# Mixing stage of a MetaFormer layer: the sum of squares on GpSimd beside VectorE's sum, and GpSimd's setup of later stages behind the stage

## The chip, the cores and the metric

One core of one Trainium2 chip. The metric is the device time of one execution in microseconds (us); a profiled execution also gives the span from the first to the last instruction.

## What is computed

x has 384 x 384 tokens with 128 channels. The layer normalises x, makes five projections of it (left, left gate, right, right gate, output gate), mixes left and right over the grid channel by channel, normalises the result over the channels, projects it, and adds it to x. A second part (an expert-choice FFN: per expert the 8 best tokens) follows.

```python
left  = (xn @ Wl + bl) * sigmoid(xn @ Wlg + blg)
right = (xn @ Wr + br) * sigmoid(xn @ Wrg + brg)
out = einsum('bkjd,bkid->bijd', left, right) / n        # per channel d: 384x384 @ 384x384
out = layer_norm(out, on_a, on_b) * out_gate            # over the 128 channels of a token
x = x + out @ Wo + bo
```

The layer norm of `out` needs, for each of the 147456 tokens, the sum and the sum of squares over the 128 channels. The change is about these two sums.

## The kernel before

The instruction streams are written by hand, one block for each engine, with semaphores between them. There are three stages and a tail.

**Stage 1** (144 steps of 1024 tokens) normalises, transposes and projects, and writes left, right and gate to DRAM by channel. GpSimd works here on normalisation (L618) and on the low parts of the input (L624).

**Mixing stage** (128 channels, buffers of two). A channel is a 384x384 map, on chip as 128 partitions x 1152 numbers. Per channel d:
- SyncE loads right and left (L485, L486), two channels ahead, when the low halves of channel d - 2 are done, and stores the mixed map (L497).
- ScalarE rounds right and left to their high parts (L811, L813). VectorE subtracts these from the whole to get the low parts (L1020, twice).
- TensorE multiplies high x high, low x high and high x low, 27 matmuls of 128x384 (L1342), into three of six PSUM banks.
- ScalarE reads the banks twice: the map itself (`mix`, L828) and its square (`mixsq`, L829). It waits first until the sums of channel d - 2 are done, since `mix` and `mixsq` have two buffers.
- VectorE adds `mix` to sum1 (L1039) and `mixsq` to sum2 (L1041). All three operands lie in SBUF.

Within a step VectorE's order is: both low halves of channel d + 1, then both sums of channel d - 1. ScalarE's order is: both casts of d + 1, then both readings of d - 1.

**Between the stages** VectorE makes mean, variance and 1/deviation out of sum1 and sum2, in three thirds of 128x384, and splits both into three bf16 parts each (L1059 to L1084). SyncE stores the parts to DRAM (L551) and loads them back broadcast for **stage 3** (L518), where TensorE applies them as outer products (L1366) and VectorE's `weighted` (L1103) begins.

**GpSimd's setup.** After stage 1 GpSimd prepares constants for what follows, each operation waiting for the one before (`alone`, which counts s_pool0): a memset and nine small loads of `exact`, then sel, half_off (two), rowsign, b2_row, pick_row, statrow (4096 bf16 in each partition, L657), coef, two affine selects on sel, one on rowsign, and two iotas (L666, L668). 17 counts in all. Then it waits for VectorE's split_rows (s_setup) and issues three loads of coef (L673). VectorE's split_rows, in the last step of the mixing stage, and SyncE's loads of gb_col and b2_row (L546, L548), behind the mixing stage and in front of the first store of the parts, both wait for all 17. During the mixing stage GpSimd does nothing.

Of the kernel before, what the change touches and what calls it, by code (L numbers as in the profile page):

```python
# [28 lines left out]
ALU = mybir.AluOpType  # L29
# [8 lines left out]
PARTS = 3  # L38
# [75 lines left out]
def build(nc, x, norm_a, norm_b, Wl, bl, Wr, br, Wlg, blg, Wrg, brg, Wog, bog, on_a, on_b, Wo, bo,  # L114
# [26 lines left out]
    with ExitStack() as ctx:  # L141
# [3 lines left out]
        def sem(name):  # L145
            return ctx.enter_context(nc.semaphore(name))
# [216 lines left out]
        s_ev = sem("s_ev")  # L363
        s_acc = sem("s_acc")
        s_mst = [sem(f"s_mst{b}") for b in range(2)]
        s_msq = sem("s_msq")
# [78 lines left out]
        N_EXACT = 3 * PARTS  # L445
        N_FIRST = 3
        N_POOL0 = 17

# [145 lines left out]
        def _(pool):  # L594
# [52 lines left out]
            for q in range(PARTS):  # L647
                pool.dma_start(exact[q:q + 1, 0, :], on_a.rearrange("(o d) -> o d", o=1)).then_inc(s_exact, 16)
                pool.dma_start(exact[PARTS + q:PARTS + q + 1, 0, :], on_b.rearrange("(o d) -> o d", o=1)).then_inc(s_exact, 16)
                pool.dma_start(exact[PARTS + q:PARTS + q + 1, 1, :], bo.rearrange("(o d) -> o d", o=1)).then_inc(s_exact, 16)  # L650
            alone(nc.gpsimd.memset(sel[:, :], 0.0))
            alone(nc.gpsimd.memset(half_off[0:EXPERTS, :], 0.0))
            alone(nc.gpsimd.memset(half_off[EXPERTS:P, :], float(CHUNK)))
            alone(nc.gpsimd.memset(rowsign[:, :], 1.0))
            alone(nc.gpsimd.memset(b2_row[:, :], 0.0))
# [4 lines left out]
            for shift in (0, EXPERTS):  # L660
                alone(nc.gpsimd.affine_select(out=sel[:, :], in_=sel[:, :], compare_op=ALU.not_equal, fill=1.0,
                                              base=-shift, pattern=[[-1, EXPERTS]], channel_multiplier=1))

            alone(nc.gpsimd.affine_select(out=rowsign[:, 0:1], in_=rowsign[:, 0:1], compare_op=ALU.is_ge, fill=-1.0,
                                          base=-PARTS, pattern=[[0, 1]], channel_multiplier=1))
            alone(nc.gpsimd.iota(place[:, :], pattern=[[1, STEPS * TOP]], base=0, channel_multiplier=0,  # L666
# [90 lines left out]
        def _(act):  # L757
# [64 lines left out]
            def evacuate(i, b):  # L822
                d = 2 * i + b
                act.wait_ge(s_mst[b], 16 * i)
                act.wait_ge(s_acc, mark(1, d - 2, 1))
                act.wait_ge(s_mix, mark(1, d, 1))
                mixed = banks[:, NT * b:NT * (b + 1), 0:GRID]
                nc.scalar.activation(mix[:, b], mixed, ACT.Copy, scale=1.0 / GRID).then_inc(s_ev, 1)  # L828
                nc.scalar.activation(mixsq[:, b], mixed, ACT.Square, scale=1.0 / GRID).then_inc(s_ev, 1)  # L829

# [105 lines left out]
        def _(dve):  # L936
# [8 lines left out]

            for s_, n in ((s_bn, 1), (s_var, 1), (s_xhat, 1), (s_prod, 4), (s_acc, 1),
                          (s_w3, 2), (s_r3, 1), (s_v3, 1), (s_m3, 2)):
                dve.sem_inc(s_, 2 * n)
# [63 lines left out]
            nc.vector.memset(sum1[:, :, :], 0.0)  # L1012
            nc.vector.memset(sum2[:, :, :], 0.0)

# [7 lines left out]
            def split_rows():  # L1022
                dve.wait_ge(s_gtp, 1)
                nc.vector.tensor_copy(gate_t[:, :], ps[7][:, 0:EXPERTS]).then_inc(s_setup, 1)
                dve.wait_ge(s_exact, 16 * N_EXACT)
                dve.wait_ge(s_pool0, N_POOL0)
                for q in range(2):
# [7 lines left out]
            def moments(i, b):  # L1035
                d = 2 * i + b
                dve.wait_ge(s_ev, mark(2, d, 1))
                dve.wait_ge(s_acc, mark(1, d - 1, 1))
                nc.vector.tensor_tensor(sum1[:, :, :], sum1[:, :, :], mix[:, b], ALU.add)  # L1039
                dve.wait_ge(s_ev, mark(2, d, 2))  # L1040
                nc.vector.tensor_tensor(sum2[:, :, :], sum2[:, :, :], mixsq[:, b], ALU.add).then_inc(s_acc, 1)  # L1041

# [12 lines left out]

            dve.wait_ge(s_acc, mark(1, DIM - 1, 1))
            for t in range(NT):
                dve.wait_ge(s_msq, t + 1)
# [422 lines left out]
```

## Time and profile before

| | us |
|---|---|
| median of 3 runs | 2883.23 (2879.32 to 2885.48) |
| profiled execution, its own time | 2879.22 |
| its span | 2877.5 |
| stage 1 | up to about 1144 |
| mixing stage, first to last addition to sum1 | 1164.59 to 1840.60 |
| stage 3 | from about 1870 to 2768 |

Times in the trace count from the start of the span. PE is TensorE's matmul, PEld its weight load, DVE is VectorE, ACT ScalarE, POOL GpSimd, SP SyncE. "L1041" is line 1041 of the kernel. Matmul ends are modelled, so a busy PE is not PE at its peak. A few per cent of the matmuls can be missing from a trace. An instruction's duration runs from its start to its end as recorded, so time that it spends waiting inside, for a port for instance, is part of it.

### The profile page before, as it was taken

The page shows a single profiled execution, that of the slowest core. Times are in us where ns is not written, and L with a number is a line of the kernel's source. Part 1 is how long each engine was busy: PE and PEld are TensorE (multiplying, and loading weights), DVE is VectorE, ACT ScalarE, POOL GpSimd, SP SyncE. Part 2 cuts the span into 40 slices and gives each one's busy share as a digit, 9 for nine tenths or more (in the row PEclk, how much of TensorE's full clock was granted, in tenths as well). Part 3 has the DMA queues.
Part 4 walks back from the last instruction along what each step waited for, and adds up shares of the span by engine and source line. Part 5 has one row for each costly group of instructions (what it writes and reads, how often), then busy time and mean ns, then how long its engine had stood idle before and what let it go on. Part 6 is the DMA issues. An engine that isn't in the chain of part 4 may idle for free.

```text
span 2877.5 us, 65085 instructions
## 1 busy us (share of the span) xinstructions
PE 2605.2 (91%) x14998; PEld 2144.7 (75%) x15070; DVE 2411.0 (84%) x4715; ACT 2254.2 (78%) x4283; POOL 1833.9 (64%) x1920
## 2 busy tenths in 40 slices
PE   7999999999999999999999999589899899988935
PEld 6888888888888887888888888566666666666623
DVE  6777777777777776999999999979899999988962
ACT  6888888888888887787778888568888888888840
POOL 7888888888888887000000000089999999999941
PEclk9999999999999999999999999789999999999978
DMA  5777777777776776999999999699999999999946
GB/s 197 273 270 266 268 273 270 268 265 272 272 269 263 272 272 248 327 332 329 320 324 332 332 331 337 229 336 374 364 365 373 366 373 365 372 355 359 365 147 214
DMA packets 281642, 873.08 MB, mean 303 GB/s; under 512 B 29710, under 2 KB 82080, under 8 KB 281600
## 3 DMA queue, kind: packets, MB, share of 16 engines
q1 hardware_dynamic: 270160, 854.87, 80.6%
q10 hardware_dynamic: 10800, 17.21, 2.0%
q0 software_dynamic: 640, 0.54, 0.2%
q8 instruction: 14, 0.23, 0.0%
q14 instruction: 28, 0.23, 0.0%
HBM read 492.97 MB, written 379.52 MB: 303 GB/s over the span
## 4 chain that ended last, share of the span: by engine, by line
PE 46%; DMA 18%; DVE 9%; issue 9%; POOL 8%; ACT 6%; SPq 3%; DVEq 1%; POOLq 0%; ACTq 0%
PE banks L1307 35%; DMA arena<-left_d 10%; DMA work<-gate_d 5%; PE banks L1296 4%; PE banks L1342 4%; POOL arena L686 3%; POOL arena L692 2%; ACT work L904 2%; PE banks L1393 2%; POOL rs L709 2%; ACT arena L828 2%; DMA work<-in_x_dram 1%; DVE bn L1123 1%; DVE arena L1114 1%; DVE arena L1041 1%
## 5 line engine op out<-in xcount | busy, mean ns | idle before, releaser
L1307 PE MATMUL banks<-x_parts,w_parts 128*128 128x512 f32 x4320 | 1067.4, 398 | 3.4 <-POOL x_parts L624 3.4
L1307 PEld LDWEIGHTS banks<-x_parts,w_parts 128*128 128x128 f32 x4320 | 791.2, 188 | 165.3 <-POOL x_parts L624 3.8
L1342 PE MATMUL banks<-left_parts,right_parts 128*128 128x384 f32 x3456 | 633.2, 342 | 58.4 <-ACT arena L829 51.0
L1342 PEld LDWEIGHTS banks<-left_parts,right_parts 128*128 128x128 f32 x3456 | 608.5, 191 | 82.8 <-issue 79.0
L982 DVE SCALAR_TENSOR_TENSOR arena<-banks,cols,arena 128x512 f32<-128x512 f32 x576 | 406.5, 747 | 247.4 <-ACT arena L794 244.3
L904 ACT ACTIVATE work<-arena,rs 128x128 f32<-128x128 f32 x1152 | 352.6, 388 | 126.6 <-POOL rs L709 126.6
L673 POOL DMA_DIRECT2D coef<-yt x3 | 1.5, 518 | 690.0 <-DVE yt L1033 690.0
L1375 PE MATMUL banks<-wo_sb,arena 128*128 128x128 f32 x2304 | 395.5, 300 | 6.3 <-DVE arena L1114 6.3
L686 POOL TENSOR_TENSOR arena<-arena,work 128x512 f32<-128x512 f32 x288 | 360.4, 1274 | 56.6 <-DVE arena L1103 56.2
L1375 PEld LDWEIGHTS banks<-wo_sb,arena 128*128 128x128 f32 x2304 | 359.9, 192 | 45.6 <-issue 16.7
L624 POOL TENSOR_TENSOR x_parts<-xn,x_parts 128x512 fp32r<-128x512 f32 x288 | 372.1, 1292 | 6.6 <-ACT x_parts L782 6.6
L618 POOL TENSOR_SCALAR arena<-arena,bn,rs 128x128 f32<-128x128 f32 x432 | 365.9, 856 | 0.5 <-POOL rs L611 0.5
L611 POOL TENSOR_TENSOR rs<-vv,mhalf 128x8 f32<-128x8 f32 x144 | 239.1, 1660 | 164.5 <-DVE vv L965 164.5
L800 ACT ACTIVATE arena<-banks,cols 128x512 f32<-128x512 f32 x288 | 198.5, 689 | 180.2 <-PE banks L1307 180.2
L1393 PE MATMUL banks<-yt,gate_t 128*64 128x512 f32 x576 | 214.0, 613 | 77.4 <-ACT yt L895 77.3
L972 DVE TENSOR_SCALAR arena<-arena,bn,rs 128x128 f32<-128x128 f32 x720 | 259.7, 438 | 5.7 <-POOL rs L611 5.4
L1376 PE MATMUL banks<-coef,statrow 128*128 128x128 bf16 x1152 | 253.4, 220 | 0.0
L709 POOL TENSOR_TENSOR rs<-vv,mhalf 128x8 f32<-128x8 f32 x144 | 237.6, 1650 | 6.5 <-DVE vv L1132 3.0
L811 ACT CAST right_parts<-arena 128x1152 fp32r<-128x1152 f32 x128 | 148.6, 1161 | 116.0 <-DMA arena<-right_d 88.4
L1103 DVE SCALAR_TENSOR_TENSOR arena<-work,cols,banks 128x512 f32<-128x512 f32 x288 | 201.0, 739 | 34.7 <-DMA work<-gate_d 19.8
L782 ACT ACTIVATE xn<-banks,cols 128x512 f32<-128x512 f32 x288 | 224.2, 779 | 2.0 <-PE banks L1296 2.0
L782 ACT ACTIVATE x_parts<-banks,cols 128x512 fp32r<-128x512 f32 x288 | 222.6, 773 | 0.0
(180 smaller groups left out, 4180.8 us busy)
## 6 DMA issues: line engine op xcount, KB each, us to landing
arena<-in_x_dram SPq DMA_DIRECT2D x144, 512.0 KB, 3.4
left_d<-arena SPq DMA_DIRECT2D x144, 512.0 KB, 2.6
right_d<-arena SPq DMA_DIRECT2D x144, 512.0 KB, 3.4
gate_d<-arena SPq DMA_DIRECT2D x144, 512.0 KB, 4.2
arena<-right_d SPq DMA_DIRECT2D x128, 576.0 KB, 5.7
arena<-left_d SPq DMA_DIRECT2D x128, 576.0 KB, 6.7
mixed_d<-arena SPq DMA_DIRECT2D x128, 576.0 KB, 4.3
work<-mixed_d SPq DMA_DIRECT2D x144, 512.0 KB, 4.8
```

The lines of the kernel that those rows point to most:

```text
L618: last = nc.gpsimd.tensor_scalar(xhat[:, b, t], xin[:, b, t], mean_of(b, t), rs[:, b, t:t + 1], ALU.subtract, ALU.mult)
L624: nc.gpsimd.tensor_tensor(x_parts[:, LO, b, c], xn[:, b, c], x_parts[:, HI, b, c], ALU.subtract).then_inc(s_lo, 1)
L686: nc.gpsimd.tensor_tensor(gated[:, b, h], gated[:, b, h], gt[:, b, h], ALU.mult).then_inc(s_g3, 1)
L709: nc.gpsimd.tensor_tensor(rs[:, b], vv[:, b], mhalf[:, 0:2 * TILES], ALU.pow).then_inc(s_n3, 1)
L782: last = nc.scalar.activation(dst, ps[c][:, :], ACT.Identity, bias=cols[:, B_COL:B_COL + 1], scale=cols[:, A_COL:A_COL + 1])
L904: last = nc.scalar.activation(ys[:, b, h, c], summed[:, b, h, c], ACT.Copy, scale=rs[:, b, k:k + 1])
L972: last = nc.vector.tensor_scalar(xhat[:, b, t], xin[:, b, t], mean_of(b, t), rs[:, b, t:t + 1], ALU.subtract, ALU.mult)
L982: nc.vector.scalar_tensor_tensor(out=dst[:, b, CHUNK * c:CHUNK * (c + 1)], in0=ps[bank][:, :], scalar=cols[:, col:col + 1], in1=sig[:, c], ...
L1307: last = nc.tensor.matmul(ps[2 + k][:, :], w_parts[:, wq, k], x_parts[:, xq, b, c], start=((wq, xq) == TERMS[0]), stop=((wq, xq) == TERMS[ ...
L1342: last = nc.tensor.matmul(ps[NT * b + t][:, 0:GRID], lr_parts[RIGHT][:, rq, b, k, t * P:(t + 1) * P], lr_parts[LEFT][:, lq, b, k], start=( ...
L1375: nc.tensor.matmul(ps[2 + h][:, tok], gated[:, b, h, tok], wo_sb[:, :], start=True, stop=False)
L1393: nc.tensor.matmul(ps[6 + b][EXPERTS * h:EXPERTS * (h + 1), :], gate_t[:, :], yt[:, b, h], start=True, stop=True).then_inc(s_l3, 1)
```

## The change

The sum of squares moves from VectorE to GpSimd, with a semaphore of its own (s_acc2); sum1 keeps s_acc. ScalarE's square of channel d waits for s_acc2 of d - 2, its plain reading for s_acc of d - 2 as before. GpSimd waits until VectorE has cleared sum2 (s_clr). The moments wait for both sums. GpSimd's setup, all but `exact` and rowsign, moves behind its 128 additions; split_rows now waits for the six counts that stand in front of them (N_ROWS), SyncE's loads of gb_col and b2_row still for all 17.

```diff
+        N_ROWS = 6
         N_POOL0 = 17
@@ GpSimd, behind the loads of exact
+            alone(nc.gpsimd.memset(rowsign[:, :], 1.0))
+            alone(nc.gpsimd.affine_select(out=rowsign[:, 0:1], in_=rowsign[:, 0:1], compare_op=ALU.is_ge, fill=-1.0,
+                                          base=-PARTS, pattern=[[0, 1]], channel_multiplier=1))
+
+            def squares(i, b):
+                d = 2 * i + b
+                pool.wait_ge(s_ev, mark(2, d, 2))
+                pool.wait_ge(s_acc2, mark(1, d - 1, 1))
+                settle(pool, s_tick_pool)
+                nc.gpsimd.tensor_tensor(sum2[:, :, :], sum2[:, :, :], mixsq[:, b], ALU.add).then_inc(s_acc2, 1)
+
+            def stage2(i):
+                for b in range(2):
+                    squares(i, b)
+
+            pool.wait_ge(s_clr, 1)
+            pairs(pool, DIM, stage2)
+
             alone(nc.gpsimd.memset(sel[:, :], 0.0))
...
-            alone(nc.gpsimd.memset(rowsign[:, :], 1.0))
...
@@ ScalarE, evacuate
                 nc.scalar.activation(mix[:, b], mixed, ACT.Copy, scale=1.0 / GRID).then_inc(s_ev, 1)
+                act.wait_ge(s_acc2, mark(1, d - 2, 1))
                 nc.scalar.activation(mixsq[:, b], mixed, ACT.Square, scale=1.0 / GRID).then_inc(s_ev, 1)
@@ VectorE
-            nc.vector.memset(sum2[:, :, :], 0.0)
+            nc.vector.memset(sum2[:, :, :], 0.0).then_inc(s_clr, 1)
...
-                dve.wait_ge(s_pool0, N_POOL0)
+                dve.wait_ge(s_pool0, N_ROWS)
...
-                nc.vector.tensor_tensor(sum1[:, :, :], sum1[:, :, :], mix[:, b], ALU.add)
-                dve.wait_ge(s_ev, mark(2, d, 2))
-                nc.vector.tensor_tensor(sum2[:, :, :], sum2[:, :, :], mixsq[:, b], ALU.add).then_inc(s_acc, 1)
+                nc.vector.tensor_tensor(sum1[:, :, :], sum1[:, :, :], mix[:, b], ALU.add).then_inc(s_acc, 1)
...
             dve.wait_ge(s_acc, mark(1, DIM - 1, 1))
+            dve.wait_ge(s_acc2, mark(1, DIM - 1, 1))
```

## Rows read from the trace of the kernel before

**Rows 1.** The page, part 1: busy us, share of the span, instructions.
```profile
PE 2605.2 (91%) x14998; PEld 2144.7 (75%) x15070; DVE 2411.0 (84%) x4715; ACT 2254.2 (78%) x4283; POOL 1833.9 (64%) x1920
```

**Rows 2.** Stretches: length; busy PE, PEld, DVE, ACT, POOL; clock, DMA share, GB/s.
```profile
1164.60:1840.60 676.00, 622.36 (x3407) 597.72 (x3406) 648.47 (x513) 547.82 (x505) 0.00 (x0) 0.98 0.94 327
1843.30:1870.00 26.70, 4.09 (x10) 1.55 (x11) 24.32 (x54) 9.20 (x20) 0.44 (x1) 0.50 0.42 146
```

**Rows 3.** Groups by line, 1150 to 1950: busy us, mean ns; idle before, releaser.
```profile
L1342 PE MATMUL banks<-left_parts,right_parts 128*128 128x384 f32 x3456 | 633.2, 342 | 58.4 <-ACT arena L829 51.0 <-ACT left_parts L813 7.0
...
L1020 DVE TENSOR_TENSOR left_parts<-arena,left_parts 128x1152 fp32r<-128x1152 f32 x128 | 173.2, 1353 | 1.1 <-ACT left_parts L813 0.5
...
L1041 DVE TENSOR_TENSOR arena<-arena 128x1152 f32<-128x1152 f32 x128 | 172.7, 1350 | 0.0
```

**Rows 4.** Timeline, VectorE, mixing stage: start us, us, engine, line, operation.
```profile
1164.59 1.35 DVE L1039 TENSOR_TENSOR arena<-arena 128x1152 f32<-128x1152 f32 x1
...
1186.21 1.35 DVE L1041 TENSOR_TENSOR arena<-arena 128x1152 f32<-128x1152 f32 x1
1187.48 1.35 DVE L1020 TENSOR_TENSOR right_parts<-arena,right_parts 128x1152 fp32r<-128x1152 f32 x1
...
1840.60 1.34 DVE L1039 TENSOR_TENSOR arena<-arena 128x1152 f32<-128x1152 f32 x1
```

**Rows 5.** Waits, 1250 to 1850: waiter, releaser, us in total, times, longest.
```profile
PE banks L1342 <- ACT arena L829: 45.3, 51, 2.6
```

**Rows 6.** Groups by line and shape, GpSimd, whole span.
```profile
L686 POOL TENSOR_TENSOR arena<-arena,work 128x512 f32<-128x512 f32 x288 | 360.4, 1274 | 56.6 <-DVE arena L1103 56.2
...
L681 POOL COPY rcol<-late 128x8 f32 x136 | 26.4, 194 | 0.0
...
L702 POOL COPY late<-mx 128x16 f32 x68 | 13.6, 200 | 0.0
...
L661 POOL TENSOR_SCALAR_AFFINE_SELECT sel<-sel 128x64 f32<-128x64 f32 x2 | 0.5, 240 | 0.3 <-POOL coef L658 0.2
...
L605 POOL TENSOR_SCALAR_AFFINE_SELECT ident<-ident 128x128 f32<-128x128 f32 x1 | 0.3, 290 | 0.2 <-POOL ident L604 0.2
```

**Rows 7.** Timeline: GpSimd and VectorE at the same time, in three places.
```profile
11.47 0.96 DVE L1001 TENSOR_TENSOR w_parts<-arena,w_parts 128x640 fp32r<-128x640 f32 x1
...
1860.23 0.56 DVE L1068 TENSOR_TENSOR arena<-arena 128x384 f32<-128x384 f32 x1
...
1860.40 0.44 POOL L681 COPY rcol<-late 128x8 f32<-128x8 f32 x1 [17.58 <-ACT late L850]
...
2770.01 1.42 DVE L1171 SCALAR_TENSOR_TENSOR late<-late,half_off 128x1152 f32<-128x1152 f32 x1 [0.95 <-ACT expo L876]
2770.78 1.44 POOL L736 TENSOR_SCALAR_AFFINE_SELECT work<-work 128x896 f32<-128x896 f32 x1
2771.47 1.37 DVE L1173 TENSOR_SCALAR late<-late,gb_col 128x1152 f32<-128x1152 f32 x1
```

**Rows 8.** Timeline: GpSimd's setup ahead of the mixing stage, and VectorE beside it.
```profile
1141.75 0.20 POOL L651 MEMSET sel<- 128x64 f32 x1
...
1142.90 3.51 POOL L657 MEMSET statrow<- 128x4096 bf16 x1
...
1144.56 1.93 DVE L1011 TENSOR_SCALAR gate_nat<-gate_nat,gsum 64x128 f32<-64x128 f32 x1
...
1147.96 1.10 POOL L666 IOTA late<- 128x1152 f32 x1
...
1149.13 2.16 POOL L668 IOTA late<- 128x1152 f32 x1
```

**Rows 9.** Timeline: behind the mixing stage, SyncE's issues and the next stage's first VectorE work.
```profile
1845.25 1.22 SPq L546 DMA_DIRECT2D gb_col<-in_L_ffn_gate_b_dram  x2
...
1854.40 0.41 SPq L551 DMA_DIRECT2D stat_d<-arena  x1
...
1870.02 1.40 DVE L1103 SCALAR_TENSOR_TENSOR arena<-work,cols,banks 128x512 f32<-128x512 f32 x2 [0.15 <-DVE arena L1069]
```

More of the change, by code:

```diff
@@ L364, in build @@
         s_acc = sem("s_acc")
+        s_acc2 = sem("s_acc2")
+        s_clr = sem("s_clr")
         s_mst = [sem(f"s_mst{b}") for b in range(2)]
@@ L662, in _ @@
                                               base=-shift, pattern=[[-1, EXPERTS]], channel_multiplier=1))
-            alone(nc.gpsimd.affine_select(out=rowsign[:, 0:1], in_=rowsign[:, 0:1], compare_op=ALU.is_ge, fill=-1.0,
-                                          base=-PARTS, pattern=[[0, 1]], channel_multiplier=1))
             alone(nc.gpsimd.iota(place[:, :], pattern=[[1, STEPS * TOP]], base=0, channel_multiplier=0,
@@ L943, in link @@
                 dve.wait_ge(s_dve, chain[0])
-            for s_, n in ((s_bn, 1), (s_var, 1), (s_xhat, 1), (s_prod, 4), (s_acc, 1),
+            for s_, n in ((s_bn, 1), (s_var, 1), (s_xhat, 1), (s_prod, 4), (s_acc, 1), (s_acc2, 1),
                           (s_w3, 2), (s_r3, 1), (s_v3, 1), (s_m3, 2)):
```

## The prediction

> **What bounds the kernel now.** I read the busy shares first [rows 1]: TensorE 91%, VectorE 84% of the 2877.5 us span. That is an average over three stages, so next comes the table by stretches [rows 2]; the mixing stage is its first line. In it VectorE is busy 648.5 of 676.0 us (96%), TensorE 92%, ScalarE 81%, the DMA engines 94%, GpSimd not at all. So three resources lie close together, and VectorE is the fullest. Then the groups of that stage [rows 3]: per channel VectorE does four additions or subtractions of 128x1152 (two low halves, the two sums), TensorE 27 matmuls (633.2 / 128 = 4.95 us). The timeline shows the additions following each other at 1.27 us (1186.21 to 1187.48), though one is listed with 1.35 [rows 4]. Four make 5.08 us. The first and the last addition to sum1 lie 1840.60 - 1164.59 = 676.0 us apart, 127 channels, so 5.32 us a channel. VectorE is 95% of that; TensorE waits for ScalarE's reading of its banks 51 times in 600 us of the stage, 45.3 us in all [rows 5].
>
> **What is removed and added in the mixing stage.** Removed from VectorE: one addition of 1.27 us in each of 128 channels; 3.81 us are left. Added on GpSimd: the same addition of 1152 elements. The trace has it only at 512 elements: 1.274 us [rows 6]. Bounds: in proportion 1152 / 512 x 1.274 = 2.87 us; with a fixed part as in GpSimd's copy of 16 elements (0.20 us, nearly all fixed), 0.20 + 1152 x (1.274 - 0.20) / 512 = 2.62 us. I take 2.62, since a fixed part is visible, and keep 2.87 as the upper end. By itself this fits twice into 5.32 us: GpSimd is idle, and nothing on its queue stands behind it.
>
> **Can the two engines add at the same time?** This decides the case, and two places of the trace speak of it [rows 7]. At 1860.40 GpSimd starts a copy of 8 elements, which takes 0.194 us elsewhere (136 times, [rows 6]); here it takes 0.44 and ends at 1860.84, just behind VectorE's subtraction of two SBUF tiles (1860.23 + 0.56 = 1860.79). At 2770.78 GpSimd starts an affine select of 896 elements. Its price from 64 elements (0.240) and 128 (0.290) [rows 6] is 0.290 + 768 x 0.00078 = 0.89 us; it takes 1.44. Had it begun to read only when VectorE's operation on two SBUF tiles ended (2771.43), it would have ended near 2772.2; it ended at 2772.22. So a VectorE instruction with two SBUF inputs keeps a GpSimd instruction that reads SBUF waiting. The other direction is less clear. At 2771.47 a VectorE operation with one input waits for the affine select (1.37 us for 1152 elements, ending 0.62 behind it). But the one subtraction with two inputs beside reading GpSimd work, at 11.47 [rows 7], took 0.96 us for 640 elements, against 0.82 on the line through 0.56 (384 elements) and 1.35 (1152): 0.14 longer.
> The Trainium skill, "SBUF — State Buffer", section "Who interferes with whom", has a rule against this change: a VectorE instruction with two SBUF inputs contends with a GpSimd instruction that reads SBUF, and whichever issues second is blocked until the first has finished. By that rule the third step below is a plain sum; by the 0.14 us of the row at 11.47 alone VectorE would lose almost nothing. The trace agrees with the rule where GpSimd is the one that waits; no row shows a long GpSimd addition against a VectorE addition.
> Whoever yields, additions that exclude each other cost their sum: 3 x 1.27 + 2.62 = 6.43 us a channel, above the 5.32 of now. With 0.05 us for each of two hand-overs (1860.84 - 1860.79) and some idling (now 5% of the period beside the fullest engine, then less, since TensorE and DMA have slack again), I take 6.65. Ends: 6.43 without any idling, and 3 x 1.27 + 2.87 + 0.10 = 6.78, with 5% idling 7.1. **Term: 127 x (6.65 - 5.32) = +169 us**; ends +141 and +226.
>
> **Waits added.** ScalarE's square of channel d now waits for GpSimd's sum of d-2; behind it on ScalarE stand the casts of a later channel, and TensorE waits for the square to free its banks. With 6.65 us a channel the sum of d-2 has a whole channel more, so this wait costs nothing unless GpSimd falls two channels back. GpSimd waits for VectorE's clearing of sum2, which comes before the first channel: nothing. VectorE's wait before the moments is now for both sums. Now the last square is followed by sum1 and sum2 (1840.60 to about 1843.2, 2.6 us); then 1.35 + 2.62 = 4.0, and up to one more 2.62 if GpSimd is a channel behind. **Term: +2 us** (0 to +5).
>
> **GpSimd's setup behind the stage.** Before the mixing stage it delayed VectorE once: a tensor_scalar of 64x128 issued at 1144.56 took 1.93 us and ended with GpSimd's memset of statrow (1142.90 + 3.51) [rows 8]. VectorE then still waits for the first channel's data, so taking that away gives nothing. Behind the stage the same operations (from 1141.75 to 1149.13 + 2.16 [rows 8], without rowsign's about 9.2 us of GpSimd) lie beside VectorE's chain of moments and splits, which fills 24.3 of 26.7 us [rows 2] and which sets the end of the stage: weighted (L1103) follows it at 1870.02 [rows 9]. The chain alternates operations with two inputs (0.56 us), which I let run beside a memset that only writes (no row shows it), with casts and tensor_scalars, which are held as the one at 1144.56 was. So the 3.51 us memset costs up to 3.51 - 0.56 = 2.9 us, and the two iotas (1.10 and 2.16 us, not shown beside VectorE) up to 0.5 and 1.6. **Term: +4.5 us** (0 if all is hidden, +9 if all is exposed).
> SyncE's queue passes its wait for the setup some 10 to 13 us behind the last sum instead of at once (L546 at 1845.25 now); six issues follow, two of which take 1.22 us, so an estimate of 3.7. The first store of the split rows (1854.40, 11.2 us behind the last sum [rows 9]) can come up to 5 us later, but the chain that makes it is itself later by 4.5, and what it feeds is needed only by L1103 at 1870.02. Nothing. The three coefficient transfers are issued behind the setup too, ahead of the first outer product: nothing. rowsign stays ahead of the stage.
>
> **Sum.** The profiled execution took 2879.2 us (span 2877.5). 2879.2 + 169 + 2 + 4.5 = 3054.7; the median of the runs lies 4.0 above the profiled one, so **3058 us**. With the ends of all terms: 2883 + 141 = 3024 to 2883 + 240 = 3123.
>
> **Rivals.**
> *They overlap (faster).* If GpSimd's addition runs beside VectorE's, as it does beside ScalarE, VectorE falls to 3.81 us, and the DMA share decides: 0.94 x 5.32 = 5.0 us, TensorE 4.95. With 5.05: 127 x -0.27 = -34, + 4.5 for the setup: about 2854 us. For it: the 0.14 us at 11.47. Against: both places where GpSimd waited to the end. It decides from the point where more than 6.43 - 5.32 = 1.1 of GpSimd's 2.62 us lie beside VectorE's additions; exactly there the time is that of now plus the setup, about 2890.
> *TensorE loses its clock, or GpSimd falls behind.* At 6.65 us a channel TensorE is busy 74%. The granted clock is 0.98 of full in the stage now, at 92% busy [rows 2]. At the lower of its two levels (1.2 GHz) 27 matmuls take some 9.9 us; with a fifth of the stage there, 127 x 0.2 x 3.25 = +83 on top: about 3140. The same follows if ScalarE comes to wait for GpSimd's sum of d-2, in whose time VectorE has nothing to add. Against: at the lower level TensorE would be busy without a break, and in the stage of now the clock comes back to a mean of 0.98.
>
> **Chances.** Additions exclude each other, 2985 to 3123: 0.74. Overlap, faster: 0.12. Overlap in part, within 2878 to 2985: 0.05. Clock or lag, above 3123: 0.09. The range must leave out no more than 0.2: 2930 to 3150 holds the first case, some 0.02 of the third and 0.04 of the last. A difference under 0.2% can't be told from none here. Faster 0.13, same 0.03, slower 0.84.
>
> **What would show it.** Right: GpSimd's additions in the mixing stage well above 2.62 us on average or VectorE's above 1.35; the fullest pair, VectorE and GpSimd, adds up to the period; DMA share and TensorE fall to about three quarters; a cast or tensor_scalar of the moments chain stretched to 3 us. Wrong: GpSimd at 2.6 to 2.9 and VectorE at 1.35 with a period near 5; or TensorE's clock well under 0.9 in the stage.

## The result and the profile after

The changed kernel takes 3006.81 us (median of 4 runs, 3005.52 to 3009.91), the kernel before, run beside it, 2884.36 us (4 runs, 2879.32 to 2890.04). The ratio is 1.0438, 95% interval 1.0417 to 1.0458: **slower by 4.4%, some 122 us**. The forecast was 3058 us, range 2930 to 3150, slower: the side and the mechanism came true, its main term was some 40% too large (+169 us against +119).

The page of after, part 1 (busy us, share of the span of 3008.2 us, instructions), against [rows 1]:
```profile
PE 2631.0 (87%) x15070; PEld 2148.2 (71%) x15070; DVE 2556.2 (85%) x4587; ACT 2254.5 (75%) x4283; POOL 2263.7 (75%) x2048
```
VectorE has 128 additions less (4587 instructions instead of 4715) and 145 us more of busy time. A VectorE instruction that GpSimd holds isn't listed as idle: it gets longer. That is the first thing to see, and a table of busy shares alone would mislead here, since VectorE looks no freer than before.

The table by stretches of after, the mixing stage (length; busy PE, PEld, DVE, ACT, POOL; granted clock, DMA share, GB/s), against the first line of [rows 2]:
```profile
1164.60:1950.00 785.40, 636.97 (x3388) 594.64 (x3387) 775.05 (x376) 544.78 (x502) 415.37 (x125) 0.98 0.82 280
```
VectorE is busy 775.05 of 785.40 us (99%, before 96%) with three additions a channel instead of four. TensorE falls from 92% to 81%, the DMA share from 0.94 to 0.82. The clock stays at 0.98.

Groups by line of after, 1150 to 2000 (busy us, mean ns; idle before, releaser), against [rows 3]:
```profile
L1360 PE MATMUL banks<-left_parts,right_parts 128*128 128x384 f32 x3456 | 651.9, 345 | 157.8 <-ACT arena L848 84.5 <-DVE left_parts L1039 36.7 <-DVE right_parts L1039 27.7
...
L663 POOL TENSOR_TENSOR arena<-arena 128x1152 f32<-128x1152 f32 x128 | 426.3, 3330 | 392.8 <-ACT arena L848 368.7 <-issue 23.7 <-POOL arena L663 0.3
...
L1058 DVE TENSOR_TENSOR arena<-arena 128x1152 f32<-128x1152 f32 x128 | 313.7, 2451 | 0.1
L1039 DVE TENSOR_TENSOR left_parts<-arena,left_parts 128x1152 fp32r<-128x1152 f32 x128 | 256.7, 2005 | 0.1
L1039 DVE TENSOR_TENSOR right_parts<-arena,right_parts 128x1152 fp32r<-128x1152 f32 x128 | 249.9, 1953 | 20.2 <-ACT right_parts L829 20.1
```
L1058 is the addition to sum1 (L1039 before), L1039 the low halves (L1020 before), L663 GpSimd's sum of squares. Each of VectorE's three kinds, 1.35 us before, now has a mean of 1.95 to 2.45 us. GpSimd's addition has a mean of 3.33 us; its shortest is 2.659 us. TensorE's matmuls are as they were (345 ns against 342); its idle time has grown from 58.4 to 157.8 us. The additions to sum1 by source line (durations in ns: shortest, median, longest; first and last start):
```profile
L1058 DVE TENSOR_TENSOR arena<-arena x128: 1337/1346/3848, 1166.0 to 1967.6; 128x1152 f32<-128x1152 f32 x128
```

The timeline of after, one meeting of the two engines (start us, us, engine, line, operation):
```profile
1315.68 1.35 DVE L1039 TENSOR_TENSOR left_parts<-arena,left_parts 128x1152 fp32r<-128x1152 f32 x1
...
1316.59 2.97 POOL L663 TENSOR_TENSOR arena<-arena 128x1152 f32<-128x1152 f32 x1 [2.05 <-ACT arena L848]
1316.94 3.84 DVE L1058 TENSOR_TENSOR arena<-arena 128x1152 f32<-128x1152 f32 x1
...
1320.70 1.35 DVE L1039 TENSOR_TENSOR right_parts<-arena,right_parts 128x1152 fp32r<-128x1152 f32 x1
```
GpSimd starts at 1316.59, while VectorE's subtraction runs until 1317.03, and ends at 1319.56. VectorE's addition starts at 1316.94, but ends at 1320.78, 1.22 us behind GpSimd's end: nearly its whole work lies behind GpSimd's. The next one, with GpSimd idle, takes 1.35 us again. First GpSimd waits for VectorE, then VectorE for GpSimd; the next additions go on at 1.27 us.

**Where the time went.** The span grew by 3008.2 - 2877.5 = 130.7 us. From start to start: the first sum1 came 1.4 later (1164.59 to 1165.98); the next 126 channels took 790.08 instead of 670.99, +119.1, that is 6.27 us a channel instead of 5.325; the last channel 11.51 instead of 5.02, +6.5; from the last sum1 to weighted 29.53 instead of 29.42, +0.1; the rest of the kernel +3.6, which is within the spread of the runs (that part is the same in all of them, and takes 1005 to 1019 us in their profiles).

### The profile page after: what moved, and what is told of

Same layout as the page of the kernel before. It is cut to its first block, busy times and chain, and to the rows that moved or that the text cites. A ratio compares the mean times of both kernels' runs of the same rounds, so it can differ in the third digit from the quotient of the medians.

```text
span 3008.2 us, 65408 instructions
## 1 busy us (share of the span) xinstructions
PE 2631.0 (87%) x15070; PEld 2148.2 (71%) x15070; DVE 2556.2 (85%) x4587; ACT 2254.5 (75%) x4283; POOL 2263.7 (75%) x2048
## 4 chain that ended last, share of the span: by engine, by line
PE 40%; issue 18%; DVE 17%; DMA 10%; POOL 8%; ACT 3%; SPq 1%; DVEq 1%; POOLq 0%; ACTq 0%
PE banks L1325 33%; DMA work<-gate_d 6%; DVE left_parts L1039 6%; DVE arena L1058 4%; PE banks L1314 4%; POOL arena L704 3%; POOL arena L710 2%; ACT work L923 2%; PE banks L1411 2%; DMA arena<-right_d 2%; DVE bn L1141 2%; POOL rs L727 1%; DVE arena L1132 1%; DMA work<-in_x_dram 1%; DVE arena L1121 1%
## 5 line engine op out<-in xcount | busy, mean ns | idle before, releaser
L1360 PE MATMUL banks<-left_parts,right_parts 128*128 128x384 f32 x3456 | 651.9, 345 | 157.8 <-ACT arena L848 84.5
L663 POOL TENSOR_TENSOR arena<-arena 128x1152 f32<-128x1152 f32 x128 | 426.3, 3330 | 392.8 <-ACT arena L848 368.7
L1058 DVE TENSOR_TENSOR arena<-arena 128x1152 f32<-128x1152 f32 x128 | 313.7, 2451 | 0.1
L1039 DVE TENSOR_TENSOR right_parts<-arena,right_parts 128x1152 fp32r<-128x1152 f32 x128 | 249.9, 1953 | 20.2 <-ACT right_parts L829 20.1
L1039 DVE TENSOR_TENSOR left_parts<-arena,left_parts 128x1152 fp32r<-128x1152 f32 x128 | 256.7, 2005 | 0.1
```

What stands on the lines that cost most here:

```text
L663: nc.gpsimd.tensor_tensor(sum2[:, :, :], sum2[:, :, :], mixsq[:, b], ALU.add).then_inc(s_acc2, 1)
L1039: nc.vector.tensor_tensor(parts[:, LO, b], whole[:, b], parts[:, HI, b], ALU.subtract).then_inc(s_lo2, 1)
L1360: last = nc.tensor.matmul(ps[NT * b + t][:, 0:GRID], lr_parts[RIGHT][:, rq, b, k, t * P:(t + 1) * P], lr_parts[LEFT][:, lq, b, k], start=( ...
```

## The experiments

The period below is that between the first and the last but one addition to sum1, over 126; before it is 5.325 us, after 6.270. Two kernels below whose stage should be as before, the setup alone and the write beside, have 5.300 and 5.294, so single profiles differ by some 0.03 us. Ratios are to the kernel before, run on the same chip, with 95% intervals.

### The two parts of the change, apart

**GpSimd's setup alone.** Both sums stay on VectorE.
```diff
...
+        N_ROWS = 6
...
+            pool.wait_ge(s_acc, mark(1, DIM - 2, 1))
             alone(nc.gpsimd.memset(sel[:, :], 0.0))
...
-                dve.wait_ge(s_pool0, N_POOL0)
+                dve.wait_ge(s_pool0, N_ROWS)
```


> Only GpSimd's setup is moved: behind the sums of channel 126, both sums stay on VectorE. Theory: GpSimd's memset of statrow (3.51 us) and the small operations beside it hold VectorE's casts and tensor_scalars in split_rows, 8.0 us instead of 2.5 in the trace of after (1959.57 to 1967.57), and nothing later: +5.5 us on the kernel before, about 2890, the mixing stage's 5.32 us a channel unchanged. Rival (the setup hides behind the stage's last waits): within 2 us of before. Rival (the prediction's place): the moments chain is longer by about 4.5 us and split_rows is not.

Measured: 2884.72 us, ratio 1.0004 (0.9985 to 1.0023), period 5.300. The timing can't tell it from no change. The trace can, in its timeline behind the stage, with the same cast in the kernel before:
```profile
1836.98 3.51 POOL L661 MEMSET statrow<- 128x4096 bf16 x1
1837.35 3.28 DVE L1033 CAST yt<-yt 6x256 bf16<-6x256 f32 x1
...
1845.28 2.28 POOL L670 IOTA late<- 128x1152 f32 x1
...
1846.06 1.71 DVE L1063 TENSOR_SCALAR arena<-arena 128x384 f32<-128x384 f32 x1
```
```profile
1839.63 0.28 DVE L1031 CAST yt<-yt 6x256 bf16<-6x256 f32 x1
```
A cast of 256 elements, 0.28 us in the kernel before, lasts until the memset of statrow ends (1837.35 + 3.28 = 1840.63 against 1840.49); a tensor_scalar, elsewhere 0.36, until 0.2 us behind the iota's end. The last channel takes 8.09 us instead of 5.02, and from the last sum1 to weighted 30.76 instead of 29.42: +4.4 us on the chain. The expectation had +5.5, all of it in split_rows; it is +3.1 there and +1.3 at the iota. The setup costs what these two rows show, and that is about the size that a comparison of medians can miss (the interval reaches to +0.23%, 6.6 us).

**The sum of squares alone.** The setup stays ahead of the stage: after, with the block of GpSimd's 128 additions put behind it.
```diff
-            pool.wait_ge(s_clr, 1)
-            pairs(pool, DIM, stage2)
-
             alone(nc.gpsimd.memset(sel[:, :], 0.0))
...
+            pool.wait_ge(s_clr, 1)
+            pairs(pool, DIM, stage2)
+
             pool.wait_ge(s_setup, 3)
```


> Only the sum of squares is moved to GpSimd; the setup stays ahead of the mixing stage. Theory (the additions of the two engines exclude each other at SBUF): 3 x 1.27 + 2.46 = 6.27 us a channel as in after, 126 x 0.95 = +120 us on the kernel before, about 3002, VectorE's stretched additions at 1.35 + 2.5 = 3.8 us. Rival (a good part of the loss comes from the setup): under +90.

Measured: 3004.13 us, ratio 1.0420 (1.0397 to 1.0442), period 6.290. Nearly the whole loss is the moved sum (4.2 of 4.4%). The last channel takes 6.06 us here, against 11.51 with the setup behind the stage.

### Is it the two engines' reading of SBUF, or the waits that were added?

**An addition beside, for which nobody waits.** The kernel before, both sums on VectorE; GpSimd makes as large an addition per channel in tiles of its own, and nobody waits for it before the stage is over (ScalarE does then, ahead of the next stage). No wait of the change is there.
```diff
...
+            def beside(i, b):
+                d = 2 * i + b
+                pool.wait_ge(s_ev, mark(2, d, 2))
+                pool.wait_ge(s_acc2, d + 1)
+                settle(pool, s_tick_pool)
+                nc.gpsimd.tensor_tensor(rstd_tok, rstd_tok, late[:, CANDS:2 * CANDS], ALU.add).then_inc(s_acc2, 1)
...
+            pairs(pool, DIM, stage2)
```


> The kernel before, in which GpSimd, idle there in the mixing stage, adds two private tiles of 128x1152 once a channel; nobody waits for it until the stage is over. Theory (exclusion at SBUF): four additions of VectorE and one of GpSimd exclude each other, 4 x 1.27 + 2.46 = 7.54 us a channel, 127 x 2.22 = +282 us, about 3166. Rival (the loss in after comes from the new waits, ScalarE's square for GpSimd's sum above all): 5.32 us a channel as before, about 2884. Rival (partial overlap): in between, 2920 to 3100.

Measured: 3164.79 us, ratio 1.0967 (1.0946 to 1.0987), period 7.541. The expectation (7.54, 3166) held to a few parts in ten thousand. Its low right halves, by source line (durations in ns: shortest, median, longest; first and last start):
```profile
L1037 DVE TENSOR_TENSOR right_parts<-arena,right_parts x128: 1342/3794/3837, 1153.3 to 2108.6; 128x1152 fp32r<-128x1152 f32 x128
```
and its stage in the table by stretches:
```profile
1166.00:2116.00 950.00, 704.56 (x3408) 643.07 (x3406) 950.00 (x503) 548.21 (x503) 402.71 (x127) 0.93 0.74 233
```
VectorE is busy all 950 us. Four additions of 1.27 and one exclusion of 2.46 are 7.54: the period is a plain sum, and the addition's cost to VectorE is the same 2.46 us as in after (6.27 - 3.81). The waits, the order and the data dependences of the change aren't needed to explain its loss.

**A write beside.** The same kernel with GpSimd writing 2304 numbers instead of adding.
```diff
-                nc.gpsimd.tensor_tensor(rstd_tok, rstd_tok, late[:, CANDS:2 * CANDS], ALU.add).then_inc(s_acc2, 1)
+                nc.gpsimd.memset(late[:, 0:2 * CANDS], 0.0).then_inc(s_acc2, 1)
```


> As the run with the private addition, but GpSimd clears 128x2304 numbers once a channel, which writes SBUF and reads nothing, for about 2.6 us. Theory (only what reads SBUF excludes VectorE's operations with two SBUF inputs): 5.32 us a channel, about 2884, VectorE's additions at 1.35. Rival (any GpSimd work in SBUF does): 4 x 1.27 + about 2.5 = 7.6 us a channel, about 3170.

Measured: 2884.90 us, ratio 1.0004 (0.9993 to 1.0015), period 5.294. By source line:
```profile
L1056 DVE TENSOR_TENSOR arena<-arena x128: 1340/1350/1358, 1164.6 to 1836.6; 128x1152 f32<-128x1152 f32 x128
...
L679 POOL MEMSET late<- x128: 2019/2032/2057, 1165.3 to 1837.1; 128x2304 f32 x128
```
128 memsets of 2.03 us hold none of VectorE's additions and subtractions (the longest of all four kinds takes 1.361 us). So for these it isn't that GpSimd works, but that it reads.

**A copy beside.** The same kernel with GpSimd copying 1152 numbers: one input instead of two.
```diff
-                nc.gpsimd.tensor_tensor(rstd_tok, rstd_tok, late[:, CANDS:2 * CANDS], ALU.add).then_inc(s_acc2, 1)
+                nc.gpsimd.tensor_copy(rstd_tok, late[:, CANDS:2 * CANDS]).then_inc(s_acc2, 1)
```


> The kernel before with a private GpSimd copy of 128x1152 numbers once a channel beside VectorE's four additions, nobody waiting for it: one SBUF input instead of two. Theory (what counts is the time in which GpSimd reads SBUF): about 1.0 us of it (1.0 to 1.3 us for the copy, less its start), 4 x 1.27 + 1.0 = 6.1 us a channel, +95 us, about 2980 (2950 to 3010). Rival (only GpSimd operations with two inputs exclude VectorE's): 2884.

Measured: 2976.74 us, ratio 1.0326 (1.0289 to 1.0362), period 6.016 = 4 x 1.27 + 0.94. GpSimd's copy by source line:
```profile
L679 POOL COPY late<-late x128: 1152/1670/2395, 1166.1 to 1925.7; 128x1152 f32<-128x1152 f32 x128
```
The shortest takes 1.152 us, of which 0.94 keeps VectorE out; of the addition's 2.659 it is 2.46. In both some 0.2 us of the instruction excludes nothing, as much as GpSimd's copy of 16 elements takes [rows 6]. The addition, with two inputs, keeps VectorE out 2.6 times as long as the copy with one; how much of this is the second input and how much the adding, no run here separates.

**A third of the addition.** After, with GpSimd adding 384 of the 1152 squares and VectorE the rest, and the setup ahead of the stage.
```diff
...
-                nc.gpsimd.tensor_tensor(sum2[:, :, :], sum2[:, :, :], mixsq[:, b], ALU.add).then_inc(s_acc2, 1)
+                nc.gpsimd.tensor_tensor(sum2[:, 0], sum2[:, 0], mixsq[:, b, 0], ALU.add).then_inc(s_acc2, 1)
...
+                nc.vector.tensor_tensor(sum2[:, 1:NT], sum2[:, 1:NT], mixsq[:, b, 1:NT], ALU.add).then_inc(s_acc, 1)
...
```


> One third of the squares' sum (384 of 1152 numbers) on GpSimd, two thirds on VectorE, setup ahead of the stage. Theory (exclusion, in proportion to the size): 3 x 1.27 + 0.87 on VectorE and 2.46 / 3 = 0.82 on GpSimd make 5.50 us a channel, with some idling up to 5.65: +22 to +42 us on before, about 2910. Rival (a fixed price for each GpSimd operation beside VectorE): as with the whole sum, over 2960. Rival (small GpSimd operations fit into VectorE's gaps): 2860 to 2885.

Measured: 2909.17 us, ratio 1.0083 (1.0058 to 1.0107), period 5.522. VectorE's 1.27 x 3 and 0.87 for the two thirds are 4.68, so 0.84 is GpSimd's: 2.46 / 3 = 0.82. The exclusion goes by the number of elements: the line through 0.84 at 384 and 2.46 at 1152 leaves 0.03 us for everything that is paid once an addition, hand-overs included. Where VectorE sets the pace, dividing the sum can't pay: each element costs VectorE about 1.1 ns if it adds it (0.87 / 768), and 2.1 ns if GpSimd does (2.46 / 1152).

### Can the exclusion be avoided?

An addition with only one input in SBUF might run beside GpSimd's. sum1's other operand lies in PSUM before ScalarE copies it, so VectorE can take it from there. Three kernels with GpSimd's sum of squares as in the change (setup ahead of the stage), and one with VectorE's.

**sum1 from PSUM, behind ScalarE's square.**
```diff
...
                 d = 2 * i + b
-                dve.wait_ge(s_ev, mark(2, d, 1))
+                dve.wait_ge(s_ev, mark(2, d, 2))
                 dve.wait_ge(s_acc, mark(1, d - 1, 1))
-                nc.vector.tensor_tensor(sum1[:, :, :], sum1[:, :, :], mix[:, b], ALU.add).then_inc(s_acc, 1)
+                nc.vector.scalar_tensor_tensor(out=sum1[:, :, :], in0=banks[:, NT * b:NT * (b + 1), 0:GRID],
+                                               scalar=1.0 / GRID, in1=sum1[:, :, :], op0=ALU.mult,
+                                               op1=ALU.add).then_inc(s_acc, 1)
...
                     pe.wait_ge(s_ev, mark(2, d - 2, 2))
+                    pe.wait_ge(s_acc, mark(1, d - 2, 1))
...
```


> Squares on GpSimd, setup ahead of the stage, and VectorE's sum1 now adds the map straight from PSUM (behind ScalarE's two readings of the banks), so that it has one SBUF input instead of two; TensorE waits for it before it writes the banks again. Theory (exclusion holds for two SBUF inputs only): sum1 runs beside GpSimd's addition at about 1.36 us (0.747 us at 512 elements with PSUM), so only 2 x 1.27 + 2.46 = 5.0 us a channel exclude each other, under the 5.0 of the DMA share: about 5.15 us a channel, -20 us on before, 2864 (2845 to 2890). Rival (every VectorE operation that writes or reads SBUF excludes GpSimd's): 6.3 us a channel, about 3005.

Measured: 2904.81 us, ratio 1.0061 (1.0037 to 1.0085), period 5.465. A miss of 0.3 us a channel, though the step that was in question came true: no addition to sum1 took over 1.359 us, and each ran beside a GpSimd addition for at least 1.1 us of them:
```profile
L1057 DVE SCALAR_TENSOR_TENSOR arena<-banks,arena x128: 1342/1357/1359, 1166.0 to 1860.1; 128x1152 f32<-128x1152 f32 x128
```
What came late is seen in its waits from 1200 to 1800 (waiter, releaser, us in total, times, longest):
```profile
ACT right_parts L829 <- PE banks L1362: 117.5, 100, 2.0
...
PE banks L1362 <- DVE arena L1057: 55.0, 103, 1.7
```
TensorE now waits for VectorE to release its banks (55.0 of 600 us), and ScalarE's casts of the next channel wait for TensorE.

**The same, with the release of the banks ahead of the next channel's halves** on ScalarE (shown) and VectorE.
```diff
...
-                    if in_range(i, b, 1, DIM):
-                        high_halves(*shifted(i, b, 1))
                     if in_range(i, b, -1, DIM):
                         evacuate(*shifted(i, b, -1))
+                    if in_range(i, b, 1, DIM):
+                        high_halves(*shifted(i, b, 1))
...
```


> As the run with sum1 from PSUM, and ScalarE and VectorE take the channel that is done (readings, sum1) ahead of the casts and low halves of the next one. Theory: TensorE's banks are free earlier and sum1 lies beside GpSimd's addition, while ScalarE makes the next casts: 5.05 to 5.2 us a channel, 2855 (2840 to 2885). Rival (the later casts hold back the loads, whose buffers are freed by the low halves): over 5.4 us a channel, over 2895. Rival (exclusion whatever the operands): about 3005.

Measured: 2968.31 us, ratio 1.0285 (1.0246 to 1.0323), period 5.980: worse, as the rival in the expectation had it. The casts come later, TensorE waits for them 102.1 us of 600, and the tiles that the loads refill come free later: 296 GB/s at a DMA share of 0.96, where before has 327 at 0.94 [rows 2]. A share of the DMA engines' time near one is no proof that they move all they can.

**sum1 from PSUM, ahead of ScalarE's two readings.** On VectorE sum1 comes ahead of the next channel's low halves.
```diff
...
-                act.wait_ge(s_acc, mark(1, d - 2, 1))
+                act.wait_ge(s_acc, mark(1, d, 1))
...
-                dve.wait_ge(s_ev, mark(2, d, 1))
+                dve.wait_ge(s_mix, mark(1, d, 1))
...
```


> As the run with sum1 from PSUM (squares on GpSimd, setup ahead), but sum1 reads the banks as soon as TensorE has filled them, in the time in which ScalarE makes the casts of the next channel; ScalarE's two readings wait for it, and TensorE waits for ScalarE alone, as in the kernel before. VectorE's order: sum1, then the low halves. Theory (the 5.47 us of the earlier run came from TensorE's wait for the late sum1; the low halves and GpSimd's addition exclude each other, 2 x 1.27 + 2.46 = 5.0): 5.0 to 5.15 us a channel, 2858 (2843 to 2878). Rival (the exclusion with the low halves, or the later readings, still costs more than the sum taken off VectorE): 5.3 us or more, 2884 or above.

Measured: 2903.44 us, ratio 1.0075 (1.0050 to 1.0100), period 5.435. Its timeline has the contrast on which this part rests:
```profile
1406.34 2.71 POOL L680 TENSOR_TENSOR arena<-arena 128x1152 f32<-128x1152 f32 x1 [2.33 <-ACT arena L848]
1406.42 1.34 DVE L1058 SCALAR_TENSOR_TENSOR arena<-banks,arena 128x1152 f32<-128x1152 f32 x1
1407.69 2.58 DVE L1039 TENSOR_TENSOR right_parts<-arena,right_parts 128x1152 fp32r<-128x1152 f32 x1
```
sum1, with one operand in PSUM, runs its 1.34 us wholly beside GpSimd's addition. The low half behind it, with both operands in SBUF, is held until GpSimd ends (1406.34 + 2.71 = 1409.05) and ends 1.22 us later. Half of GpSimd's addition is hidden, yet the kernel isn't faster than before, as the rival in the expectation had it: in 600 us of the stage VectorE is busy 522, TensorE 545, and the DMA share is 0.94.

**The same order, with the sum of squares on VectorE.**
```diff
...
-                nc.vector.tensor_tensor(sum1[:, :, :], sum1[:, :, :], mix[:, b], ALU.add)
+                nc.vector.scalar_tensor_tensor(out=sum1[:, :, :], in0=banks[:, NT * b:NT * (b + 1), 0:GRID],
+                                               scalar=1.0 / GRID, in1=sum1[:, :, :], op0=ALU.mult,
+                                               op1=ALU.add).then_inc(s_acc, 1)
+
+            def second(i, b):
...
+                nc.vector.tensor_tensor(sum2[:, :, :], sum2[:, :, :], mixsq[:, b], ALU.add).then_inc(s_acc2, 1)
...
```


> The same order with sum1 from PSUM, but both sums on VectorE (sum2 behind the low halves), GpSimd idle in the mixing stage. VectorE does 1.36 + 3 x 1.27 = 5.17 us a channel. Theory: 5.25 to 5.35 us a channel as before, 2884 (2870 to 2892), so that what the run beside it gains is GpSimd's doing. Rival (the order alone is the gain): under 2865.

Measured: 2895.46 us, ratio 1.0050 (1.0033 to 1.0068), period 5.382: somewhat slower than was expected. So half to two thirds of what the kernel with the earlier reading loses against before (0.057 of 0.110 us a channel, 0.50 of 0.75%) it loses by this order and the reading from PSUM, without GpSimd. In this order too, moving the sum to GpSimd gains nothing.

### What would a freed VectorE be worth at all?

**No sum of squares.** The kernel before without the addition to sum2, on either engine (its output lacks the variance): the best that the change could have reached in this stage.
```diff
-                nc.vector.tensor_tensor(sum1[:, :, :], sum1[:, :, :], mix[:, b], ALU.add)
-                dve.wait_ge(s_ev, mark(2, d, 2))
-                nc.vector.tensor_tensor(sum2[:, :, :], sum2[:, :, :], mixsq[:, b], ALU.add).then_inc(s_acc, 1)
+                nc.vector.tensor_tensor(sum1[:, :, :], sum1[:, :, :], mix[:, b], ALU.add).then_inc(s_acc, 1)
```


> The kernel before without the sum of squares: VectorE adds to sum1 alone and nobody adds to sum2 (ScalarE still squares), so it shows what taking that addition off VectorE is worth if GpSimd cost nothing; the output lacks the variance. VectorE has 3.81 us a channel. The prediction's price of the case of overlap: 5.05 us a channel, -34 us, 2850 (2840 to 2865). Rival (two load buffers go round in 10.6 us: 6.7 us of loading, a cast of 1.16, a subtraction of 1.35, issue; none of this gets shorter): 5.25 to 5.32 us a channel, 2875 to 2884.

Measured: 2878.52 us, ratio 0.9984 (0.9967 to 1.0001), period 5.238. Its stage in the table by stretches:
```profile
1164.60:1836.00 671.40, 619.75 (x3418) 591.70 (x3416) 505.43 (x395) 554.73 (x513) 1.54 (x3) 0.99 0.94 331
```
and two of its waits:
```profile
DVE right_parts L1020 <- ACT right_parts L811: 145.2, 115, 3.2
...
ACT right_parts L811 <- DMA arena<-right_d: 73.2, 80, 2.6
```
VectorE is down to 75% and waits for ScalarE's casts, and those for the loads; the period falls by 0.09 us, not by 1.27 (by 0.06 against the two kernels at 5.294 and 5.300). VectorE's 96% in the kernel before was not what set 5.3 us; or rather, a second limit lies less than 0.1 us under it.

**Is it the order of SyncE's queue?** A store of the mixed map waits there between the loads. The kernel before with the stores issued by GpSimd.
```diff
...
-                    if in_range(i, b, -1, DIM):
-                        store_mixed(*shifted(i, b, -1))
...
+            def store_mixed(i, b):
+                pool.wait_ge(s_ev, mark(2, 2 * i + b, 1))
+                pool.dma_start(mixed_w[2 * i + b], mix[:, b]).then_inc(s_mst[b], 16)
...
+            pairs(pool, DIM, stage2)
...
```


> The kernel before, both sums on VectorE, but the stores of the mixed maps are issued by GpSimd instead of SyncE, so that a load no longer stands behind a store that waits for ScalarE (in the trace of before SyncE waits 329.7 us of 600 for that reading; a load follows its free buffer by 0.8 us at 1301.49, low halves done at 1300.73). Theory (the two load buffers going round, 10.6 us for two channels, set the period, with or without the second sum): 0.3 to 0.4 us a channel less, 5.0 to 5.1, about 2852 (2845 to 2868). Rival (the DMA engines are full at a share of 0.94, or VectorE at 95%): 5.25 to 5.32, 2875 to 2884. Rival (GpSimd's issue is slower than SyncE's and the maps' buffers are freed late): over 2890.

Measured: 2929.31 us, ratio 1.0155 (1.0128 to 1.0182), period 5.652, where a shorter one was expected: wrong. Its DMA issues from 1200 to 1800 (count, KB each, median us from issue to landing):
```profile
mixed_d<-arena POOLq DMA_DIRECT2D x106, 576.0 KB, 8.1
arena<-right_d SPq DMA_DIRECT2D x105, 576.0 KB, 6.5
arena<-left_d SPq DMA_DIRECT2D x105, 576.0 KB, 7.9
```
In the kernel before the same three take 4.4, 5.7 and 6.7 us. With the stores out of the way SyncE waits 477.3 us of the 600 for low halves (7.8 us at the longest; 9.5 us in all before), that is for tiles to come free, and the loads land later. That the stores cause this is argued, not shown. The time lies where the last rival had it, but its reason isn't seen: ScalarE waits 1.9 us in the whole stage for a store. Nor is the run a clean test of the queue's order, since the stores also change their kind of queue: the profile lists them under q0 software_dynamic (14985 packets, 25.0% of the engines' time), where before all went through q1 hardware_dynamic. What sets the floor of 5.2 to 5.3 us, the loop of loads and the tiles that they refill or what the DMA engines can move, stays open. The chain that ended last points to the loads: from 1200 to 1800 those of left are 42.7% of it before, and 61.0% without the sum of squares. A kernel with a third tile for each operand would tell, and it wasn't tried. No version faster than the kernel before was found.

## Why the prediction was right, and where not

**What bounds the stage: wrong in one step.** "VectorE is the fullest" was right as a row [rows 2]; to take it for the limit was not. Without the sum of squares the stage gains less than 0.1 us a channel. The forecast didn't rest on this, but the rival "they overlap (faster)" did: it took 0.94 x 5.32 = 5.0 us as the DMA engines' need, and -34 us as its price. The share stays 0.94 at 5.24 us a channel, with VectorE at 75%. Measured, even an addition that costs nothing is worth 0.16%, at most 0.33% by the interval, which reaches to nothing; the rival's true price was a sixth to a third of the one given (5.7 us by the medians, 11 by the periods of the two profiles).

**The two engines exclude each other: right, and shown.** GpSimd's addition that nobody waits for costs VectorE 2.46 us a channel, a memset nothing, a copy 0.94, and an addition with an operand in PSUM isn't held. The rows from which it was argued [rows 7] showed, for VectorE's work with two inputs, only GpSimd waiting; the direction that was "less clear", VectorE waiting for GpSimd, is the one of 57 of the 128 additions to sum1 in after (about 3.83 us each; the other 71 take 1.35). The 0.14 us of the row at 11.47 was a poor guide: it gave VectorE almost no loss. GpSimd's three tensor_scalars beside it (9.89 to 13.10) have 128 elements each, a ninth of the addition's, and the exclusion goes by elements.
The rule of the Trainium skill ("SBUF — State Buffer", "Who interferes with whom") held in each part that these runs show: two inputs in SBUF contend with a GpSimd instruction that reads (2.46 us), not with one that only writes (1.350 us median, unheld), an addition with one input in SBUF, outside what the page calls the 2-port modes, not at all (1.359 us at most), and whoever issues second waits until the other has finished (the timeline at 1316.59). Not every VectorE instruction with one input goes free: the casts and tensor_scalars that a memset and an iota held (3.55 and 1.71 us) have one input too.

**The size: +169 forecast, +119 measured.** The term was 6.65 = 3.81 + 2.62 + 0.10 (two hand-overs) + 0.12 (idling) a channel; the period is 6.27 = 3.81 + 2.46. GpSimd's addition was well estimated, 2.62 against 2.66 for the shortest, but VectorE is kept out for only 2.46, hand-overs included. How much of that is hand-over the period alone can't say; the run with a third of the addition leaves at most some 0.03 us. Idling, carried over from the 5% of the kernel before, adds nothing: VectorE is 99% busy, and its 10 us of idle time in the stage all lie beside GpSimd's additions. The three errors are 0.16, 0.10 and 0.12 us, 48 us over 127 channels. The lower end of +141 left out idling and hand-overs but not the first error, so the measured term lies under it, and the time under the sum's own ends (3024 to 3123); the range held it because it reached further down, to the partial case.

**Waits added: right in after, in part by luck.** In the last channel the sum1 of channel 126 is held, where an unheld sum1 and sum2 stood before (+1.0), and GpSimd's last addition holds VectorE's two tensor_scalars of split_rows (2.81 instead of 0.58, +2.2); against that, no sum2 stands behind the last sum1 (-1.2). That is +2.0; +2 was forecast, though with GpSimd behind sum1, where it came ahead of it. With the sum alone moved the same two stretches give +1.0 and -1.2, that is -0.2: there the sum1 of channel 126 isn't held, and GpSimd's last addition holds a cast of split_rows for 2.58 us instead of 0.28. The two parts apart add up to 4.4 - 0.2 = 4.2 us, both together cost 6.6, so the +2.0 hangs on which instructions happen to meet. ScalarE's square never waits for GpSimd's sum: no such row is among the waits from 1250 to 1900, and the lag of the last rival didn't come.

**GpSimd's setup: right in size, wrong in place.** The timeline of after at the end of the stage:
```profile
1958.59 3.52 POOL L663 TENSOR_TENSOR arena<-arena 128x1152 f32<-128x1152 f32 x1 [0.17 <-POOL arena L663]
...
1959.70 2.81 DVE L1047 TENSOR_SCALAR yt<-yt,rowsign 6x128 f32<-6x128 f32 x2
...
1963.21 3.51 POOL L677 MEMSET statrow<- 128x4096 bf16 x1
1963.31 3.55 DVE L1050 CAST yt<-yt 6x256 bf16<-6x256 f32 x1
...
1967.57 1.34 DVE L1058 TENSOR_TENSOR arena<-arena 128x1152 f32<-128x1152 f32 x1
...
1970.25 2.30 POOL L686 IOTA late<- 128x1152 f32 x1
...
1971.06 1.71 DVE L1079 TENSOR_SCALAR arena<-arena 128x384 f32<-128x384 f32 x1
```
The memset of statrow was put beside the moments. It holds a cast of split_rows (3.55 instead of 0.28, +3.3), which stands ahead of the last sum1; beside the moments one iota holds one tensor_scalar (+1.35). Together 4.6 us against 4.5 forecast, and 4.4 with the setup moved alone. That casts and tensor_scalars are held by a memset, as at 1144.56 [rows 8], while additions are not, was right: a memset holds a cast here again, and 128 memsets beside additions cost nothing. The stage's end is 6.5 + 0.1 = 6.6 us later by both terms, 2.0 + 4.6.

**The clock: that rival didn't come.** At 6.27 us a channel TensorE is busy 81% and its granted clock is 0.98, as before. The rival's own case of TensorE busy 74% came in the run with the private addition, at 7.54 us a channel: the clock is 0.93 there, and the period is still the plain sum.

**What was to be seen.** GpSimd's additions above 2.62 (mean 3.33) and VectorE's above 1.35 (1.95 to 2.45): yes. VectorE and GpSimd adding up to the period: yes as 3.81 + 2.46, not in the busy times as listed (775 and 415 of 785 us), which count the waiting too. TensorE and DMA share at about three quarters: 0.81 and 0.82, as the shorter period has it. A stretched cast or tensor_scalar of about 3 us: yes, one place earlier.

## What to carry to other kernels

Before work is moved from VectorE to GpSimd, count where the operands of both lie: with two inputs in SBUF on VectorE and a GpSimd instruction that reads SBUF, the times add, and GpSimd's is the longer one (2.46 us against 1.27 for the same 1152 elements a partition). A GpSimd memset goes beside VectorE's additions, though not beside its casts, and a VectorE addition with one operand in PSUM goes beside GpSimd's. And before an engine is relieved, leave the work out once: relieving VectorE at 96% busy was worth at most 0.33%, because the next limit lay less than 2% lower (5.238 against 5.325 us a channel).

## What the runs showed of the hardware that was not expected

- Excluding costs no more than the excluded work: VectorE and GpSimd took turns 128 times at 3.81 + 2.46 = 6.27 us, and the run with a third of the addition (0.84 us against 2.46) leaves at most some 0.03 us for hand-overs.
- About 0.2 us of a GpSimd instruction excludes nothing (2.659 - 2.46 for the addition, 1.152 - 0.94 for the copy).
- What GpSimd does sets the price: 0.94 us of exclusion for a copy of 1152 elements, 2.46 for an addition of as many.
- A memset of 3.51 us held a cast of 256 elements for 3.3 us, and memsets of 2.03 us held no addition: what a VectorE instruction loses beside a GpSimd memset depends on its kind, and can be many times its own length (0.28 us).
- Stores issued by GpSimd took 8.1 us to land instead of 4.4, and the loads of SyncE's queue beside them took 0.8 to 1.2 us longer.
